# A transformer block with attention between two feed-forward layers: one tile product of the feed-forward and one bias addition change places

## The reference

```python
def ffn(x, w1, b1, w2, b2):                 # 256 -> 1024 -> 256
    return gelu(x @ w1 + b1) @ w2 + b2      # exact gelu
def attn(x, w_qkv, w_out, b_out):           # 16 heads of 64
    q, k, v = heads(x @ w_qkv)
    sim = (q * 64**-0.5) @ k.T - abs(i - j) * slope[head]   # causal
    return softmax(sim) @ v @ w_out + b_out
x = x + 0.5 * ffn(layernorm(x), w1, b1, w2, b2)
x = x + attn(layernorm(x), w_qkv, w_out, b_out)
x = x + 0.5 * ffn(layernorm(x), w1, b1, w2, b2)
```

## Time and profile before

| | before |
|---|---|
| median of 3 runs | 2199.65 us |
| the profiled execution | 2198.49 us |
| its span, first to last instruction | 2196.7 us |
| mean granted TensorE clock | 0.991 of full |
| PE busy | 2144.5 us (98%) |
| DVE busy | 1506.4 us (69%) |
| ACT busy | 1234.8 us (56%) |
| POOL busy | 1070.2 us (49%) |

### The profile page before, as it was taken

The page is one execution under the profiler, slowest core; times in us unless marked ns, Lnnn a source line. Parts: engine busy times, 40 slices in busy tenths (PEclk is TensorE's granted clock), DMA queues, the critical chain, the costliest instruction groups (busy, mean ns, idle before and its releaser), DMA issues.

```text
span 2196.7 us, 41801 instructions
## 1 busy us (share of the span) xinstructions
PE 2144.5 (98%) x14720; PEld 1741.3 (79%) x14720; DVE 1506.4 (69%) x4011; ACT 1234.8 (56%) x3096; POOL 1070.2 (49%) x1773
## 2 busy tenths in 40 slices
PE   5999999999999999999999999999999999999998
PEld 5678787887878778787887878878787787878866
DVE  7666766758676676766767667686766767667664
ACT  4654736557364564646547365573646646465471
POOL 3653826537174462735538265371744627355371
PEclk8999999999999999999999999999999999999998
DMA  3331504325052340513415043250523405133151
GB/s 129 103 100 36 152 26 127 86 64 137 13 143 70 85 128 8 157 49 106 107 34 154 25 125 88 65 139 10 146 67 87 126 9 156 49 107 106 34 144 35
DMA packets 109985, 193.91 MB, mean 88 GB/s; under 512 B 34512, under 2 KB 53200, under 8 KB 109776
## 3 DMA queue, kind: packets, MB, share of 16 engines
q1 hardware_dynamic: 89296, 138.77, 22.5%
q0 software_dynamic: 20480, 52.47, 9.7%
HBM read 14.95 MB, written 8.39 MB: 11 GB/s over the span
## 4 chain that ended last, share of the span: by engine, by line
PE 87%; ACT 4%; POOL 4%; DVE 3%; issue 1%; SPq 1%; DMA 0%; DVEq 0%; POOLq 0%; ACTq 0%
PE ps L283 85%; POOL P L942 3%; ACT P L604 2%; PE ps L337 2%; ACT L604 1%; DVE P L787 1%; SPq L229 1%; ACT qk L564 1%; DVE x L734 0%; DVE gl L705 0%; POOL PT L229 0%; DVE gh L754 0%; DMA raw<-in_L_ffn_w 0%; DMA PT<-P 0%; DVE xtl L705 0%
## 5 line engine op out<-in xcount | busy, mean ns | idle before, releaser
L942 POOL TENSOR_SCALAR P<-P,rs 128x512 f32<-128x512 f32 (+3 forms) x1024 | 540.8, 547 | 439.0 <-DVE rs L770 435.6
L604 ACT ACTIVATE P<-P,mx 128x512 f32<-128x512 f32 (+3 forms) x1024 | 562.5, 552 | 196.6 <-DVE mx L779 196.5
L229 POOL DMA_DIRECT2D PT<-P x640 | 322.7, 509 | 240.9 <-DVE P L787 222.4
L787 DVE STREAM_TRANSPOSE P<-P 128x1792 f32<-128x1792 f32 (+1 forms) x256 | 374.0, 1485 | 12.4 <-POOL P L942 11.8
L283 PE MATMUL ps<-qk 64*128 64x512 f32 (+3 forms) x2048 | 312.2, 444 | 4.5 <-ACT qk L564 4.5
L283 PE MATMUL ps<-PT,v 128*64 128x256 f32 (+1 forms) x3072 | 307.9, 350 | 6.1 <-DMA PT<-P 3.8
L283 PE MATMUL ps<-w2h,gh 128*128 128x256 f32 x1024 | 294.7, 288 | 6.6 <-DVE gl L705 6.4
L283 PE MATMUL ps<-w2l,gh 128*128 128x256 f32 x1024 | 290.9, 284 | 0.0
L283 PE MATMUL ps<-w2h,gl 128*128 128x256 f32 x1024 | 290.7, 284 | 0.0
L283 PEld LDWEIGHTS ps<-PT,v 128*64 128x64 f32 x3072 | 205.0, 138 | 103.4 <-issue 13.2
L564 ACT ACTIVATE qk<-ps 128x512 f32<-128x512 f32 x256 | 153.0, 598 | 231.7 <-PE ps L283 231.7
(11 more groups left out here) (83 smaller groups left out, 4411.6 us busy)
## 6 DMA issues: line engine op xcount, KB each, us to landing
PT<-P SPq DMA_DIRECT2D x1408, 80.0 KB, 2.6
PT<-P POOLq DMA_DIRECT2D x640, 80.0 KB, 2.7
x<-in_L_attn_x SPq DMA_DIRECT2D x16, 512.0 KB, 4.3
out_y<-x SPq DMA_DIRECT2D x15, 512.0 KB, 3.2
raw<-in_L_ffn_w SPq DMA_DIRECT2D x2, 512.0 KB, 5.9
raw<-in_L_ffn_w SPq DMA_DIRECT2D x1, 1024.0 KB, 8.6
rawq<-in_L_attn_w_qkv SPq DMA_DIRECT2D x1, 1024.0 KB, 6.7
rawk<-in_L_attn_w_qkv SPq DMA_DIRECT2D x1, 1024.0 KB, 8.8
```

What stands on the lines that cost most here:

```text
L229: e.dma_start(PT[c % 2][32 * m:32 * m + 32, g, :], P[c % 3][32 * g:32 * g + 32, m, :]).then_inc(landed[c % 3].sem, 16)
L604: e.activation(p, p, ACT.Exp, bias=mx[:, r, i:i + 1], scale=-1.0, accum_out=sm[:, r, i:i + 1]).then_inc(s_ex.sem, 1)
L787: e.transpose(p, p).then_inc(s_tr.sem, 1)
L942: e.tensor_scalar(p, p, rs[:, 2 * (c % 2) + h, i:i + 1], 1.0, ALU.mult, ALU.mult).then_inc(s_nz.sem, 1)
```

## The change

Two places are edited. In TensorE's `begin`, dn(2) now stands between k2 and q2, and not behind q2. In GpSimd's `attention`, the bias addition for the next batch is issued after the normalising of pair 7 (`NC - 1`) and not after that of pair 6 (`NC - 2`); in both cases it stands ahead of that pair's DMA issues.

```diff
@@ begin(b) on TensorE
                 proj_tile(b, ("k", 2))
+                if b > 0:
+                    dn(2, b - 1, 2)
                 proj_tile(b, ("q", 2))
                 if b > 0:
-                    dn(2, b - 1, 2)
                     dn(2, b - 1, 3)
@@ attention(b) on GpSimd
                     if b + 1 < NB:
                         if c == 4:
                             power(1, b + 1)
-                        if c == NC - 2:
+                        if c == NC - 1:
                             bias(1, b + 1)
                     spread(e, b, c, SPREAD_POOL, s_pp)
```

## The result

The kernel after took 2220.17 us, the median of 6 runs (2211.92 to 2224.59), beside 2199.61 us for the kernel before (6 runs, 2198.49 to 2200.42). The ratio is 1.009, with a 95% interval of 1.0073 to 1.0106: slower by 0.9%, 20.6 us. The forecast was slower by 11.4 us. Runs of the kernel before lie within 2 us of each other, those of the kernel after within 12.7. A time that scatters so is a finding of its own, and it leads to the cause.

What follows compares the result with a forecast made beforehand. TensorE was taken as the bound. The first edit counted 0, the second 14 x 0.81 = 11.4 us; 2198.49 + 11.4 = 2209.9 profiled, plus 1.16 for the median: 2211 us, range 2204 to 2216.

Steps and rivals of the forecast that it cites:

- The first edit at nothing: TensorE's begin: dn(2) ahead of q2 only moves the 0.47 and 0.10 us stall; taken as 0, bounds -8.6 to +1 us.
- nothing behind it is late: Begin, behind dn(2): dn(3) has 0.8 us cover, q2's copy is 2 us early, the exps fit ScalarE's idle time.
- No gain from the old place: GpSimd, 1063.81 to 1066.17: the addition filled a gap of waiting for VectorE's transposes, so removing it frees nothing.
- gl(1) held up for the rest of the addition: VectorE's subtraction gl(1) waits out GpSimd's addition, ending 1.10 us late; TensorE's dn(0) loses 0.8 us a batch.
- The slack of the first batch: Batch 0: dn(0) starts 7.2 us after GpSimd's normalising in place of 6.15; 1.0 us more slack covers the delay.
- The 11.4 us of the sum: Second edit's whole cost: 14 batches at 0.81 us in TensorE's dn(0).
- gl(1) waits for 1077.41: VectorE's gl(1) waits until the moved addition ends at 1077.41, then ends at 1077.95 in place of 1076.85.
- the bounds, 2205 to 2216: Contention case's range: 2205 if the late half is worth half, 2216 at 1.2 us a batch; chance 0.80.
- No contention: Rival: gl(1) slowed only 0.2 us, swallowed by ScalarE's slack; both edits cost nothing, 2199.7 us; chance 0.12.
- a gain in `begin`: Rival: the stall ahead of q2 goes, 15 x 0.57 = 8.6 us faster, 2191 us; chance 0.03.
- late DMAs: Rival: pair 7's DMAs issue 1.1 us late and its values wait; price 0, or 2228 at 2 us a batch; chance 0.01.
- The case of a small cost: Rival: the addition covers gl(1) by 0.3 us only; 14 x 0.2 us, 2202.5 us; chance 0.04.

Runs made afterwards that it cites:

- e1_dn_only: Kernel before with only dn(2) moved ahead of q2, the bias addition left at its old place: 2199.0 us, ratio 0.9997.
- e2_bias_only: Kernel before with only the bias addition moved behind pair 7's normalising, TensorE's order unchanged: 2212.2 us, ratio 1.0061.
- r2_after: Kernel after, unchanged, run once more in another session and on another chip: 2213.2 us, ratio 1.0062 to the kernel before.
- e10_forced: Kernel after with VectorE made to wait for the bias addition before gh(0) in every batch: 2247.2 us, ratio 1.0223.
- e3_quarters: Kernel after with the bias addition issued as four GpSimd instructions of 128x256 in place of one: 2216.5 us, ratio 1.0073.
- e5_halves: Kernel after with half of the bias addition left at the old place and half at the new one: 2198.7 us, ratio 0.9998.
- e9_best: Kernel before with add3(b-1, 1) ahead of pair 0's first transpose and GpSimd waiting for gh(0) inside pair 7's normalising: 2193.5 us, ratio 0.9976.
- e8_gap: Kernel after with GpSimd waiting for gh(0) between pair 7's fifth and sixth normalising instructions: 2205.7 us, ratio 1.0034.

## Why the prediction was wrong

**The first edit at nothing: right.** The wait of 0.47 us and the restart moved from q2 to dn(2), unchanged, 15 times; e1_dn_only is the same as before within 0.1%. That nothing behind it is late held too.

**No gain from the old place: right.** The bias addition's old gap was free: in e2_bias_only the rest outside dn(0) is 2198.2 us, as in the kernel before.

**gl(1) held up for the rest of the addition: right in mechanism and size.** 1.10 us late was forecast, 1.1 to 1.2 measured (1.71 to 1.82 us for gl(1), less 0.64); 0.81 us a batch was forecast, 0.73 a batch measured in e2_bias_only (10.2 us in 14 batches), where no batch missed its turn. The slack of the first batch held against this. The 11.4 us of the sum are 10.2 in that profile.

**The step that failed** is the choice of the one VectorE instruction that the addition meets. The forecast set "gl(1) waits for 1077.41" and took gh(0) and gl(0) as they were before, because both were through when the addition began. They were through because gh(0) had got the port at the end of one normalising instruction. That is no right of the copy but a turn that it wins mostly: in the profile before it missed the turns behind the fifth and the sixth instruction in one of the 15 batches, the 13th. There it took 1.47 us and got the port only as the seventh ended, and the eighth was stretched from 0.47 to 0.63 us; dn(0) lost 0.26 us. The rows of VectorE and GpSimd in the kernel before:

```profile
1739.34 1.47 DVE L754 CAST gh<-gt 128x512 fp32r<-128x512 f32 x1 [1.82 <-ACT gt L582]
```

GpSimd's eighth instruction:

```profile
1740.51 0.63 POOL L942 TENSOR_SCALAR P<-P,rs 128x256 f32<-128x256 f32 x1
```

The addition at its new place stands in the same queue without a gap, so a copy that goes on missing its turns waits for it too, 2.4 us more, and the batch loses 3.0 us in place of 0.75. The four such batches of the profile lost 11.2 us, 8.2 more than at 0.75 each; the profiled execution is 19.7 us over before where 11.4 were forecast, so this is, in the main, what the forecast lacks. With gl(1) alone, as in the profiled run of e2_bias_only (2208.36 us), the time lies inside the range.

A number of missed turns that changes from run to run also makes the time scatter, and the three profiles with 0, 2 and 4 go with it. It is not shown to be the whole of the scatter: no run of the kernel after above 2218.23 us was profiled, and the granted clock varies too, from 0.988 to 0.992 in the kernel after (0.988 in the run of 2223.71 us). The gh(0) of 1.47 us stood in the timeline of the kernel before and was not read; the bounds, 2205 to 2216, had only gl(1) in them and were too narrow for that reason.

**The rivals.** No contention and a gain in `begin` are out. So are late DMAs: TensorE waited for PT 5.8 us in all after and 3.8 before, but 2.3 in e2_bias_only, which has the same move. The case of a small cost, in which the bias addition covers gl(1) by 0.3 us only, is out as well: it was held up 1.1 us or more in the profile after.

**A small rest.** In the tenth batch, behind the waits of dn(0), TensorE's granted clock fell from its level of 2.4 GHz to 1.2 for 3.4 us; the other three batches with a missed turn show no fall there. The row of the stretch has its length, the busy time of PE, PEld, DVE, ACT and POOL, then the granted clock, the DMA share and GB/s:

```profile
1361.00:1368.00 7.00, 5.78 (x29) 5.19 (x30) 3.65 (x8) 2.25 (x4) 0.60 (x2) 0.76 0.57 155
```

The mean of 0.76 over 7 us is about half the time at the lower level. From the start of its dn(0) to that of the next batch are 137.7 us, where those of its like have 135.6 to 136.2, so such a fall costs 1.5 us or more. Between the setup and the end, falls inside a dn(0) or at its end stand only in batches whose gh(0) came behind the addition: one of four here, one of two in r2_after (the 12th batch), two of 15 in e10_forced (the first and the ninth). One more fall, at 127 to 128 us, is in these two runs and in e3_quarters, e5_halves and e9_best, and has nothing to do with gh(0), which comes later.

**What stays open** is why gh(0) misses its turn in one batch and not in another. It asks 0.36 us before the fifth normalising instruction ends in both, to within 0.02 us. Open too are why the same kernel took 2220.2 us in the first session and 2213.2 in the second, why the wait of e8_gap works as it does, and what the runs of e3_quarters above 2215 us hold.

## What to carry to other kernels

A gap on GpSimd is not free because GpSimd is idle in it: list what VectorE asks for while the instruction stands there, and also what has asked before and may still be waiting, since a back-to-back row of GpSimd instructions can shut out a waiting VectorE instruction to its very end. One instruction in a long row of like ones that took twice as long, in one batch of 15, is the trace's notice that a race is being won by luck. A wait of GpSimd for the VectorE instruction, placed inside the row, took the luck out in two kernels, in all 15 batches of each profile; look in the trace at which instruction then gives way, since it was not the one that was meant. And before a scatter in time is put down to a cause, look at the granted clock of each run.

## What the runs showed of the hardware that was not expected

The shared port of VectorE and GpSimd is not handed to the one who has waited longer. gh(0) waited through three more normalising instructions and the whole of the bias addition, 4.26 us, while GpSimd's eight instructions took 4.09 us, nearly the 4.07 of e10_forced, where gh(0) does not ask beside them. In other batches it got its turn at the first boundary. The Trainium skill, page "SBUF — State Buffer", section "Who interferes with whom", says that whoever issues first gets the shared pair for the whole instruction and the other blocks. For an instruction in work this holds here, in all but e8_gap and e9_best, where gh(0) went ahead of an instruction whose row begins within 0.03 us of its own. For the next turn the order of asking does not decide: the quarter that began at 278.16 held off a subtraction that had asked at 277.98.
